# Macaron block with ternary FFNs: the second block's tokens prepared in the weight phase, A's tokens sooner, the last block's chain partly on VectorE

## The reference

```
x = x + 0.5 * ffn(layernorm(x))         # "A"
x = x + attention(layernorm(x))         # "B": 32 heads of 16, window 128, softmax, Wq Wk Wv Wo
x = x + 0.5 * ffn(layernorm(x))         # "C", same weights as A

ffn(y):  gate, up = split(y @ ternary(w_gate_up).T)     # 2 x 2048
         h = silu(gate) * up
         return (h * rsqrt(mean(h*h) + eps)) @ ternary(w_proj).T
```

## Time and profile before

| | |
|---|---|
| median of 3 runs | 2096.93 us (2095.19 to 2098.56) |
| the profiled execution | 2096.15 us, of it a span of 2094.4 us |
| granted TensorE clock, mean of the span | 0.974 |
| busy share PE, DVE, ACT, POOL | 94%, 81%, 66%, 39% |
| instructions in the span | 61719 |

### The profile page before, as it was taken

How to read it: one execution, slowest core, us unless ns; L and a number is a source line. 1 busy time by engine, 2 the same in 40 slices (tenths; PEclk the granted TensorE clock), 3 DMA queues, 4 the chain that set the end, 5 groups by cost and what they waited for, 6 DMA issues and landing times. The chain is left out here.

```text
span 2094.4 us, 61719 instructions
## 1 busy us (share of the span) xinstructions
PE 1958.8 (94%) x24751; PEld 1429.4 (68%) x25008; DVE 1692.2 (81%) x4398; ACT 1376.2 (66%) x2361; POOL 807.0 (39%) x693
## 2 busy tenths in 40 slices
PE   6477799999999999999999999999999999999777
PEld 4355577777777777777777777777777777777465
DVE  7956788778887888878887888878887888878773
ACT  7735677666766667666766676667666667666562
POOL 1032344444344344444344444443434444433222
PEclk9788899999999999999999999999999999999889
DMA  6314667566675567656674567657764567656650
GB/s 213 135 30 72 114 103 117 99 103 115 114 122 89 100 113 112 112 92 113 121 122 79 99 117 125 107 85 119 122 110 87 101 116 122 106 84 113 116 102 21
DMA packets 760879, 222.24 MB, mean 106 GB/s; under 512 B 745744, under 2 KB 745744, under 8 KB 760080
## 3 DMA queue, kind: packets, MB, share of 16 engines
q1 hardware_dynamic: 760592, 218.26, 58.6%
HBM read 25.17 MB, written 8.39 MB: 16 GB/s over the span
## 5 line engine op out<-in xcount | busy, mean ns | idle before, releaser
L636 ACT ACTIVATE masked<-masked,exp_bias,exp_scale 128x256 f32<-128x256 f32 (+1 forms) x1024 | 501.6, 562 | 40.9 <-DVE exp_bias L850 40.9
L931 PE MATMUL ps_gu<-xt_A,wgu_t 128*128 128x128 f16 x8192 | 486.3, 221 | 17.2 <-DMA xt_A<-xh 10.6
L931 PEld LDWEIGHTS ps_gu<-xt_A,wgu_t 128*128 128x128 bf16 x8192 | 473.0, 99 | 41.9 <-DMA xt_A<-xh 10.8
L931 PE MATMUL ps_gu<-xt_C,wgu_t 128*128 128x128 f16 x8192 | 481.7, 220 | 9.2 <-DMA xt_C<-xh 9.2
L931 PEld LDWEIGHTS ps_gu<-xt_C,wgu_t 128*128 128x128 bf16 x8192 | 466.9, 99 | 18.0 <-DMA xt_C<-xh 9.4
L785 DVE CUSTOM_DVE_ANT_0 masked<-ps_s,mask 128x256 f32<-128x256 f32 (+1 forms) x1024 | 337.3, 385 | 0.8 <-PE ps_s L967 0.7
L759 DVE TENSOR_TENSOR prob<-masked,prob 128x1024 f16<-128x1024 f32 (+1 forms) x256 | 309.8, 1210 | 9.4 <-ACT prob L659 9.2
L541 ACT ACTIVATE h_hi<-hid 128x512 f16<-128x512 f32 x256 | 160.7, 628 | 232.8 <-DVE hid L774 213.4
L512 POOL TENSOR_TENSOR acc_A<-acc_A,sq 128x512 f32<-128x512 f32 x96 | 126.7, 1320 | 434.0 <-ACT sq L653 434.0
L759 DVE TENSOR_TENSOR h_lo<-hid,h_hi 128x512 f16<-128x512 f32 x256 | 198.2, 774 | 114.0 <-ACT h_hi L541 111.3
L512 POOL TENSOR_TENSOR acc_C<-acc_C,sq 128x512 f32<-128x512 f32 x96 | 122.6, 1277 | 385.8 <-ACT sq L653 385.8
(11 more groups left out here) (161 smaller groups left out, 2284.7 us busy)
## 6 DMA issues: line engine op xcount, KB each, us to landing
stream<-in_L_attn_x_dram SPq DMA_DIRECT2D x32, 256.0 KB, 2.9
pt<-prob SPq DMA_TRANSPOSE x512, 3.2
out_dram<-stream SPq DMA_DIRECT2D x32, 256.0 KB, 2.6
stream<-in_L_ffn_w_gate_up_dram SPq DMA_DIRECT2D x4, 1024.0 KB, 5.4
prob<-in_L_ffn_w_gate_up_dram SPq DMA_DIRECT2D x4, 1024.0 KB, 5.8
stream<-in_L_ffn_w_proj_dram SPq DMA_DIRECT2D x2, 1024.0 KB, 5.2
prob<-in_L_ffn_w_proj_dram SPq DMA_DIRECT2D x2, 1024.0 KB, 5.0
wv<-in_L_attn_Wo_dram SPq DMA_DIRECT2D x1, 1024.0 KB, 7.8
```

What stands on the lines that cost most here:

```text
L636: t = act.activation(p, p, ACT.Exp, bias=exp_bias[:, 4 * g + h:4 * g + h + 1], scale=exp_scale[:, 0:1])
L931: t = pe.matmul(bank[:, j * P:(j + 1) * P], wgu_t[:, k, at:at + P], xt[s][:, part, k, :], start=(k == 0 and part == 0), stop=(k == KD - 1 ...
```

## The change

- `LN_A, XHAT_A, SPLIT_A` go from -5, -4, -2 to -6, -5, -4: statistics and `norm_apply` one step sooner, the split and its DMA two steps. The load of x hangs on `LN_A` and moves by one step with it.
- Block 1's A tokens no longer pass through the steps: DVE takes the statistics after unit 8 of the weights, POOL does `power`, `norm_apply` and `low` after the maximum of Wv and Wo, ACT copies at half unit 23, SP transposes before the loads of x blocks 2 and 3.
- Last block: O's projection goes to the head of PE's step 271, `add_output` and the statistics to DVE's step 271 ahead of `gated`; the output's split (step 270) goes ahead of tanh on ACT and of `gated` on DVE; `rstd` on POOL in step 271, `xhat` on DVE in step 271 after `hidden`, the remainder on DVE too; ACT's copy and SP's DMA in step 272.
- Last sum of squares: POOL leaves out the last chunk's addition and both folds, PE makes eight products with `ones` instead of one.

```diff
-    LN_A, XHAT_A, SPLIT_A = -5, -4, -2
+    LN_A, XHAT_A, SPLIT_A = -6, -5, -4
+    LAST_WO = 8 * LAST + WO_AT
+    LAST_SPLIT = LAST_WO + 1
...
+        def in_steps(s, b):
+            return b > 1 if s == "A" else s == "B" or b < LAST
...
 (SP, weight phase)
             sp.dma_start(at_raw[K], at_units[K]).then_inc(a_in[K], 16)
+            normalised_t("A", 1, p_up["A"], 8)
 (SP, steps)
+                if step == LAST_SPLIT:
+                    sp.wait_ge(d_xl, 1)
+                    sp.wait_ge(p_up["C"], 8 * LAST)
+                    transpose(xt["C"][:, :, :, :].rearrange("p a b c -> p (a b) c"), flat(xh[:, :, :]), t_x["C"])
...
 (POOL, weight phase)
             pool.partition_all_reduce(w_max[:, V:O + 1], w_abssum[:, V:O + 1], P, RMAX).then_inc(a_all, 1)
+            power(rstd["A"], var_eps["A"], d_ve["A"], g_rstd["A"], 1)
+            norm_apply("A", 1)
+            low(xh[:, 1, :], xhat[:, :], xh[:, 0, :], a_xh["A"], 2, g_xl["A"])
 (POOL, steps)
-                if s and c > 0:
+                last = s == "C" and bf == LAST and c == 3
+                if s and c > 0 and not last:
...
+                if step == LAST_WO:
+                    power(rstd["C"], var_eps["C"], d_ve["C"], g_rstd["C"], LAST)
...
 (ACT, weight phase)
+                if i == 23:
+                    act.wait_ge(t_x["A"], 16)
+                    copy(xh[:, 0, :], xhat[:, :], g_xh["A"], 2, a_xh["A"])
 (ACT, steps)
+                if step == LAST_SPLIT:
+                    split_free(act, step, "C")
+                    copy(xh[:, 0, :], xhat[:, :], d_xh, 1, a_xl)
+                if block_at(step, SPLIT_O) == LAST:
+                    output_hi(LAST)
                 s, b, c = ffn_at(step)
                 if s and not (s == "A" and b == 0):
                     tanh_half(s, b, c, step)
...
 (DVE, weight phase)
+                if n == NGU:
+                    norm_stats("A", 1, x_in[1], 16)
 (DVE, steps)
+                if block_at(step, SPLIT_O) == LAST:
+                    output_lo(LAST)
+                if step == LAST_WO:
+                    add_output(LAST)
+                    norm_stats("C", LAST, d_x2, NB)
                 s, bf, c = ffn_at(step)
                 first = s == "A" and bf == 0
                 if s and not first:
                     gated(s, bf, c, step)
...
+                if step == LAST_WO:
+                    dve.wait_ge(g_rstd["C"], NB)
+                    xhat_free(dve, LAST_SPLIT - 1)
+                    dve.tensor_scalar(xhat[:, :], slot(LAST), mean_var["C"][:, 0:1], rstd["C"][:, 0:1],
+                                      ALU.subtract, ALU.mult).then_inc(d_xh, 1)
...
                     take_lo(h_lo[:, step % 3, :], hid[:, step % 2, :], h_hi[:, step % 3, :], a_hh[s], 4 * bf + c + 1,
                             d_hl[s])
+                if step == LAST_WO:
+                    take_lo(xh[:, 1, :], xhat[:, :], xh[:, 0, :], a_xl, 1, d_xl)
...
 (PE)
+            def last_square_sum():
+                pe.wait_ge(g_acc["C"], 3 * LAST + 2)
+                for n, squares in enumerate((acc["C"][:, :], sq[:, (8 * LAST + UP_C + 3) % 2, :])):
+                    if n == 1:
+                        pe.wait_ge(a_sq["C"], 4 * NB)
+                    for j in range(4):
+                        t = pe.matmul(ps_sq, squares[:, j * P:(j + 1) * P], ones[:, :], start=(n == 0 and j == 0),
+                                      stop=(n == 1 and j == 3))
+                t.then_inc(p_sq["C"], 1)
...
             def step_of(step):
+                if step == LAST_WO:
+                    output_projection(LAST)
```

More of the change, by code:

```diff
@@ L39, in macaron @@
     NB = B * S // P
+    LAST = NB - 1
     BPS = S // P
@@ L513, in step_of @@
                                        op=ALU.add).then_inc(g_acc[s], 1)
-                if s and c == 3:
+                if s and c == 3 and not last:
                     pool.wait_ge(g_acc[s], 3 * bf + 3)
@@ L523, in step_of @@
                     b = block_at(step, offset)
-                    if b is not None and (s != "A" or b > 0):
+                    if b is not None and in_steps(s, b):
                         low(xh[:, 1, :], xhat[:, :], xh[:, 0, :], a_xh[s], b + 1, g_xl[s])
@@ L618, in step_of, with output_hi @@
                     b = block_at(step, offset)
-                    if b is not None and (s != "A" or b > 0):
+                    if b is not None and in_steps(s, b):
                         split_free(act, step, s)
                         copy(xh[:, 0, :], xhat[:, :], g_xh[s], b + 1, a_xh[s])
+                if step == LAST_SPLIT:
+                    split_free(act, step, "C")
+                    copy(xh[:, 0, :], xhat[:, :], d_xh, 1, a_xl)
+                def output_hi(b):
+                    need(act, t_o, 16 * b)
+                    copy(oh[:, 0, :], o_norm[:, :], d_on, 4 * b + 4, a_oh)
+                if block_at(step, SPLIT_O) == LAST:
+                    output_hi(LAST)
                 s, b, c = ffn_at(step)
@@ L626, in step_of @@
                 b = block_at(step, SPLIT_O)
-                if b is not None:
-                    need(act, t_o, 16 * b)
-                    copy(oh[:, 0, :], o_norm[:, :], d_on, 4 * b + 4, a_oh)
+                if b is not None and b < LAST:
+                    output_hi(b)
                 b, g = group_at(step, SCORES)
@@ L873, in step_of, with output_lo, add_output @@
                     normalise_o(b, g // 2)
+                def output_lo(b):
+                    take_lo(oh[:, 1, :], o_norm[:, :], oh[:, 0, :], a_oh, b + 1, d_ol)
+                def add_output(b):
+                    dve.wait_ge(p_wo, b + 1)
+                    dve.scalar_tensor_tensor(out=slot(b), in0=ps_m[:, :], scalar=out_scale[:, 0:1], in1=slot(b),
+                                             op0=ALU.mult, op1=ALU.add).then_inc(d_x2, 1)
+                if block_at(step, SPLIT_O) == LAST:
[3 more added lines that the diff above has]
+                    norm_stats("C", LAST, d_x2, NB)
                 s, bf, c = ffn_at(step)
@@ L880, in step_of @@
                 b = block_at(step, WO_AT + 1)
[L881 to L884, removed]
+                if b is not None and b < LAST:
+                    add_output(b)
                 if s:
@@ L908, in step_of @@
                 b = block_at(step, LN_C)
-                if b is not None:
+                if b is not None and b < LAST:
                     norm_stats("C", b, d_x2, b + 1)
                 b = block_at(step, LN_A)
-                if b is not None and b > 0:
+                if b is not None and in_steps("A", b):
                     norm_stats("A", b, x_in[b % 2], 16 * (b // 2 + 1))
@@ L1114, in step_of @@
                 b = block_at(step, WO_AT)
[L1115 to L1119, removed]
+                if b is not None and b < LAST:
+                    output_projection(b)
                 for n in weight_halves(step, 0):
```

21 lines of the change are left out of this document (15 added, 6 removed).

## The result

The changed kernel takes 2108.31 us (median of 5 runs, 2107.66 to 2110.39) against 2096.93: a ratio of 1.0060, 95% interval 1.0046 to 1.0073. It is slower, by 11.4 us in the medians. The profiled execution was the slowest of the five, 2110.39 us with a span of 2108.6.

A forecast was written before the change was run, and what follows sets the result against it. PE was taken as the bound, busy 94% of the span, with waits at start and end and no slack in step mod 7. Terms summed to +13.0 on 2096.15 us: 2109.2 us, range 2088.5 to 2113.5.

The forecast's parts named there:

- term 1: Weight phase: making block 1's tokens there costs 1.01 us of DVE statistics plus 0.6 beside POOL's `low`, +1.6 us.
- term 2: Step 8: the 7.49 us wait goes, Q's projection starts 2.2 sooner but runs up to 2.3 slower; -0.3 us.
- term 3: Step 16: PE's 3.07 us wait for A's tokens goes, -3.0 us; steps 20 to 24 add +0.3.
- term 4: Middle, step mod 4: POOL's `low` starts just ahead of DVE's `prob` and delays it, so PE waits; +18.5 us.
- term 5: Last block: output's DMA and C chain come sooner, shortening PE's wait of 8.74 us; -4.1 us (-2.5 to -5.5).
- term 6: Last sum of squares: eight products on PE take 1.8 us and end at the same time; 0 (-0.4 to +1).
- Wide blocks: 14 middle blocks with a 1024-column `prob`: POOL leads by 0.05 us, DVE loses 0.98 us in each.
- narrow ones: 7 middle blocks with a 512-column `prob`: it would take 1.66 instead of 0.98 us, +0.68 in each.
- the seven others: 7 middle blocks where DVE leads in step mod 4: POOL waits, 1.54 instead of 0.56 us, and DVE loses nothing.
- Rival (a): No collision in the middle: a tenth's shift puts DVE first and it loses nothing; -6.5, 2089.7 us; chance 0.30.
- (b): Half a collision in the middle: only wide blocks, 2104.4 us (chance 0.08), or only narrow, 2095.5 us (0.07).
- (d): Start gives its 7.5 us: Q's projection not late and at full speed, 2 us less; inside the forecast's 0.50.

The follow-up runs named there:

- run 1: Changed kernel with POOL's `low` for A waiting until DVE has written that step's low half of `prob`: 2098.56 us, ratio 1.0013 to the kernel before.
- run 5: Changed kernel with A's split alone back at -2, statistics and `xhat` left at -6 and -5: 2092.11 us, 0.9984 of the kernel before.
- run 6: Changed kernel with A's low half made by POOL in two instructions of 256 columns instead of one of 512: 2098.53 us, ratio 1.0009 to the kernel before.
- run 9: Changed kernel with POOL's `low` for A waiting until DVE has written that step's `o_norm`: 2092.45 us, 0.9974 of the kernel before.
- run 4: Kernel before with only block 1's tokens made in the weight phase: 2098.96 us, ratio 1.0014.
- run 7: Changed kernel with block 1's tokens made in the steps again, at the new offsets: 2102.63 us, ratio 1.0035 to the kernel before.
- run 10: Changed kernel with `low` for A waiting for `o_norm` and block 1's tokens made in the steps again: 2086.64 us, 0.9951 of the kernel before.
- run 2: Kernel before with the last block's part of the change alone, including the last sum of squares in eight products: 2091.05 us, ratio 0.9975.
- run 3: Kernel before with the three offsets of A alone (-6, -5, -4), block 1's tokens still made in the steps: 2107.94 us, ratio 1.0057.

## Why the prediction was right, and where it was off

The forecast was 2109.2 (2088.5 to 2113.5); measured 2108.31. The range was wide and had both signs in it; what the forecast committed itself to was "slower", at 0.60 against 0.30 for "faster". Against the profiled execution of before the sum was +13.0, and the trace, of the slowest execution, has +14.2. Term by term, forecast and trace:

| term | forecast | trace |
|---|---|---|
| 1 weight phase | +1.6 | +2.7 |
| 2 step 8 | -0.3 | +0.8 |
| 3 step 16; steps 17 to 24 | -3.0; +0.3 | -3.0; +0.4 |
| 4 the middle | +18.5 | +17.6 |
| 5 last block | -4.1 | -4.4 |
| 6 last sum of squares | 0 | +0.1 |

That the total is off by 0.9 us only is in part luck: terms 1 and 2 were low by 1.1 each, terms 4 and 5 high by 0.9 and 0.3, and the rest is the difference between executions. The mechanism is not luck: it is in the trace where the forecast has it.

*Term 4* decided the sign, and it came from a row: a pair 0.05 us apart on a step without slack. Wide blocks lose 7.10 - 6.13 = 0.97 each (forecast 0.98), narrow ones 6.87 - 6.33 = 0.54 (forecast 0.68), the seven others nothing. In the narrow ones DVE did lose 0.68 at `prob`, but by the `o_norm` that PE waits for it was only 0.55 late (15.97 us from the one to the other before, 16.52 now): 0.66 late up to the next step's `h_lo`, it is 0.57 late at the `sq_mean_A` behind it and 0.54 from there on, so it had some 0.1 us of waiting there that I had not taken off. Runs 1, 5, 6 and 9 take the hold away, move it or halve it, each in another way, and the middle follows each time: +8.8, -0.5, +7.7 and +0.1 us against before, where the changed kernel has +17.6. Rival (a), the lead lost by a tenth, did not come true: the lead of 0.04 to 0.05 held in both kinds of blocks, and so neither case of (b) did either. (d) is ruled out by the rows of the start: the projection was late and slow. What I had not seen is that "POOL second" would not have been free either: run 1 shows `low` behind `prob` holding `o_norm`, and so do the seven blocks of the changed kernel in which DVE leads, where "DVE loses nothing" was wrong by 0.34 us (0.75 in one) and only their slack hid it. That reading rested on a one-column instruction, which is done before `o_norm` begins. With `low` in its place rival (a) would have stood between about 2094 and 2098 instead of 2089.7, by my estimate: 14 wide blocks at that 0.34, or the 8.8 us of run 1.

*Term 1* was low by 1.1. The statistics took 1.01 as forecast. I gave POOL's part 0.6, at one hold by `low`; there were two, 0.46 beside `xhat` and 0.96 by `low`, the latter on an instruction with one input. My text counted none for `xhat`. The Trainium skill ("SBUF — State Buffer", Who interferes with whom) says that `tensor_scalar` can enter the modes that use both ports and then contends with GpSimd. The 1.65 in place of 0.69 agrees; the 0.69 beside `xhat` in run 4 shows that it isn't always VectorE that waits. The remaining 0.3 us lies ahead of the statistics, where nothing was changed, and is the difference of two executions.

*Term 2* was the weakest step: "2.2 sooner, up to 2.3 slower". The projection started 1.7 us sooner, reckoned from the end of the longer weight phase (141.01 + 2.74 against 142.05), and took 2.55 longer (5.30 against 2.75). I had named both sizes and then taken less than the second, when the row said that all of the slow stretch moves. And I had it on both sides: the "about 5 us" of idle PE count A's chunk as slow still, while it ran in 3.73 and the wait was 6.96. The 0.5 missing from "2.2 sooner" arose ahead of step 8: `w_pow` took 1.50 in place of 0.92, and from it on VectorE is 3.3 us late and not 2.74. From there B's chain did come 1.9 us sooner, as forecast (its DMA at 138.90 is 1.43 later than the 137.47 of before). What that 0.5 hangs on stays open: run 5, the same code up to there, has `w_pow` at 0.17 and starts step 9 as late, 3.6 us after before. And I costed this part only against the kernel before. The better comparison is run 7 (and run 10 against run 9): with the offsets moved anyway, making block 1 in the weight phase is a loss of 5 to 6 us.

*Terms 3, 5 and 6* held. In term 5 the low half was held by POOL's last addition, as written: 1.34 us at 2075.15. The eight products of term 6 take 1.84 us (forecast 1.8) and end where the fold's one product ended. Runs 2 and 4 gave these parts alone about what they have in the sum. Runs 3 and 4 do not add up to the changed kernel, since both remove the wait of step 8.

## What to carry to other kernels

Before moving a GpSimd instruction, write down what VectorE starts within a few tenths of its new place, and whether that step has slack downstream: here a lead of 0.04 us in 21 blocks cost more than two removed waits and a shorter tail gained. If it must move, place it beside VectorE instructions that read one operand from PSUM (two such were not held in run 9), not merely behind the one it collided with. A wait that occurs once or twice should be mended in those iterations alone. And when a wait goes, ask what PE does next and at which clock: work that fills the slow stretch while something else is late is free, a pause in its place puts the slow stretch on the critical chain.

## What the hardware showed that I had not expected

- The hold goes by instruction, and the next in line gets its turn: in run 6 POOL's second piece, issued at once, let `prob` through and was held 1.0 us itself (1.65 against the 0.67 of the first).
- The kind of POOL instruction matters. Beside `xhat` (2.67 us at 96.03) a product with two inputs lost 0.46 us, and in run 4 a `tensor_scalar` lost nothing, while `low` (1.21) held the same `tensor_scalar` for 0.96. What sets the share of `xhat` I did not test.
- The same 64 matmuls of step 8 took 3.73 us in the changed kernel and 6.19 in run 7, and the 12 of the projection 5.30 and 2.76; the sum is nearly the same (9.03 and 8.95), and what counts is which of the two the slow clock after the wait falls on.
